# When the weighted sums of the last phase start, and how the first gathers leave

## The reference, cut to what matters

```
scores  = softmax(xt @ Wg.T)                      # 16 experts
topi    = the 4 best experts of the 2 best groups # per token
weights = scores at topi
h   = silu(xt @ W1[e].T) * (xt @ W3[e].T)         # expert e, 352 wide
y   = sum over the 4 chosen e of weights * (h @ W2[e].T)
z   = silu(xt @ Ws1.T) * (xt @ Ws3.T) @ Ws2.T     # shared, 704 wide
out = x + y + z
```

## Time and profile before

| | |
|---|---|
| median of 3 runs | 918.76 us (918.58 to 924.74) |
| the profiled execution | 918.96 us, of which the span is 917.4 us |
| PE busy | 898.6 us, 98% of the span |
| DVE busy | 555.3 us, 61% |
| POOL busy | 494.6 us, 54% |
| ACT busy | 332.5 us, 36% |
| TensorE clock granted | 1.000 over the span |
| in the last phase, 825.65 to 900.85 us | PE busy 75.20 of 75.20 us, DVE 71.00, POOL 56.64 |
| landing of `hblk<-h_d` after its issue | 2.6 us (median of 79) |

### The profile page before, as it was taken

The page is one execution under the profiler, slowest core; times in us unless marked ns, Lnnn a source line. Parts: engine busy times, 40 slices in busy tenths (PEclk is TensorE's granted clock), DMA queues, the critical chain, the costliest instruction groups (busy, mean ns, idle before and its releaser), DMA issues.

```text
span 917.4 us, 19372 instructions
## 1 busy us (share of the span) xinstructions
PE 898.6 (98%) x4966; PEld 804.3 (88%) x4967; DVE 555.3 (61%) x1104; ACT 332.5 (36%) x708; POOL 494.6 (54%) x346
## 2 busy tenths in 40 slices
PE   8999998899999999999999999999999999999998
PEld 5777887688889999999999999999999999989997
DVE  6656667988886644444444444444444444459996
ACT  4556554454324322333323333333333333332221
POOL 1127777874167774434646664456666643137771
PEclk9999999999999999999999999999999999999999
DMA  6729996655579977777878776778878755588883
GB/s 217 259 105 377 392 402 256 230 191 171 185 234 304 304 246 200 226 198 241 254 237 250 250 246 200 236 244 252 256 247 252 250 166 157 162 243 249 269 259 128
DMA packets 180649, 218.97 MB, mean 239 GB/s; under 512 B 56576, under 2 KB 124160, under 8 KB 180224
## 3 DMA queue, kind: packets, MB, share of 16 engines
q1 hardware_dynamic: 118080, 123.50, 42.2%
q0 software_dynamic: 20816, 79.44, 26.2%
q10 hardware_dynamic: 41712, 15.54, 6.3%
HBM read 127.38 MB, written 91.03 MB: 238 GB/s over the span
## 4 chain that ended last, share of the span: by engine, by line
PE 80%; DVE 9%; issue 4%; ACT 3%; DMA 2%; POOL 1%; ACTq 0%; DVEq 0%; SPq 0%; POOLq 0%
PE ps L1173 15%; PE ps L1174 15%; PE ps L1175 15%; PE ps L1232 8%; PE ps L1230 8%; PE ps L1231 8%; PE ps L1022 2%; PE ps L1038 2%; PE ps L969 1%; DVE st L1479 1%; DVE res L1477 1%; PE ps L1058 1%; PE ps L1060 1%; PE ps L1059 1%; DVE st L1294 1%
## 5 line engine op out<-in xcount | busy, mean ns | idle before, releaser
L1173 PE MATMUL ps<-whi,xhi 128*128 (+1 forms) x888 | 287.9, 324 | 1.5 <-DVE xlo L1522 0.8
L1175 PE MATMUL ps<-whi,xlo 128*128 (+1 forms) x888 | 286.0, 322 | 0.0
L1174 PE MATMUL ps<-wlo,xhi 128*128 (+1 forms) x888 | 285.9, 322 | 0.0
L1554 DVE TENSOR_TENSOR hrow<-ps,sg 128x352 f32<-128x352 f32 x95 | 49.8, 524 | 217.8 <-ACT sg L841 212.1
L1173 PEld LDWEIGHTS ps<-whi,xhi 128*128 128x128 f32 x888 | 166.9, 188 | 6.2 <-issue 1.4
L1174 PEld LDWEIGHTS ps<-wlo,xhi 128*128 128x128 f32 x888 | 167.0, 188 | 4.0
L1175 PEld LDWEIGHTS ps<-whi,xlo 128*128 128x128 f32 x888 | 166.6, 188 | 0.0
L841 ACT ACTIVATE sg<-ps 128x352 f32<-128x352 f32 x111 | 51.6, 465 | 275.2 <-PE ps L1175 275.2
L848 ACT ACTIVATE xhi<-ps 128x512 fp32r<-128x512 f32 x112 | 67.0, 598 | 141.2 <-DVE ps L1515 141.1
L569 POOL TENSOR_TENSOR wlo<-raw,whi 128x2816 fp32r<-128x2816 f32 x16 | 100.6, 6289 | 2.4 <-POOL whi L567 0.8
L661 POOL DMA_INDIRECT raw<-yslot_d,sloti x64 | 68.3, 1067 | 55.3 <-DMA yslot_d<-ysb 22.6
(11 more groups left out here) (204 smaller groups left out, 1579.8 us busy)
## 6 DMA issues: line engine op xcount, KB each, us to landing
raw<-wexp_in POOLq DMA_DIRECT2D x18, 2176.0 KB, 11.1
xslot_d<-zero SPq DMA_DIRECT2D x10, 2048.0 KB, 21.5
xg<-xslot_d SPq DMA_DIRECT2D x320, 64.0 KB, 2.1
yslot_d<-ysb SPq DMA_DIRECT2D x80, 256.0 KB, 2.4
h_d<-hrow ACTq DMA_DIRECT2D x79, 192.0 KB, 2.9
hblk<-h_d SPq DMA_DIRECT2D x79, 192.0 KB, 2.6
xg<-xn_d SPq DMA_DIRECT2D x128, 64.0 KB, 3.4
xq<-x_in SPq DMA_DIRECT2D x16, 256.0 KB, 3.3
```

What stands on the lines that cost most here:

```text
L1173: pe.matmul(ps[:, bank, 0:INTER], xh, wh, start=(k == 0), stop=False)
L1174: pe.matmul(ps[:, bank, 0:INTER], xh, wl, start=False, stop=False)
L1175: mm = pe.matmul(ps[:, bank, 0:INTER], xl, wh, start=False, stop=(k == KT - 1))
```

## The change

`LAG` goes from 1 to 0 and `PACE` from 9 to 8: sums 4t to 4t+3, those of tile t, stand in step t, one in each quarter, from step 0 to step 15. On POOL the gathers of tiles 1 to 3 no longer wait until those of the tile before have landed. The gathers of tiles 4 to 15 keep their waits: for the matmuls of `up` three tiles back, and for the sums that free their ring place.

```diff
-LAG, PACE = 1, 9
+LAG, PACE = 0, 8
...
             for t in range(NT):
-                if 1 <= t < GR:
-                    pool.wait_ge(gathered[t - 1], 16 * TOPK)
                 if t >= GR:
                     pool.wait_ge(mm1, 2 + NT + NR + t - 2)
                     pool.wait_ge(comb, TOPK * (t - GR + 1))
```

## The result

The changed kernel takes 922.43 us (median of 22 runs, 919.69 to 926.4), the kernel before, in as many runs beside it, 920.38 us (917.38 to 924.74). The ratio is 1.0026, with a 95% interval of 1.0014 to 1.0037: about 2.4 us slower (the two medians lie 2.05 us apart). The forecast was 1.4 us over the kernel before, whose first three runs had a median of 918.76; with more runs that median moved up by 1.6 us, which has nothing to do with the change.

What follows compares the result with a forecast made beforehand. PE, busy 98% of the span, was taken to set the pace. Profiled 918.96 + 0 + 0 + 1.4 = 920.4 us; with the runs' median 0.2 us lower, the forecast was 920.2 us, range 918.5 to 922.5.

Steps and rivals of the forecast that it cites:

- Middle steps, 0 us: Steps 1 to 14: four sums a step relieve DVE, but PE has no idle time to give back; 0 us.
- Gathers in time for their sums, 0 us: Last phase, tiles 0 to 3: gathers land before their sums want them, all with 5 us or more to spare; 0 us.
- Step 15, +1.4 us: End of last phase: the chain of sums on DVE delays h_low(15), so down(15) starts late; +1.4 us, at least +0.9.
- Step 0, 0 us: Start of last phase: four new sums fit DVE's idle time and PE's slack, so they cost nothing; 0 us.
- the transfers of routed tile 78 land late: Rival near step 0: more gathers in flight slow tile 78's store and load, PE waits 2.9 us, 923.1 us; chance 0.12.
- The rule of the Trainium skill: On the tile 78 rival: engines alternate between queues, so a deeper gather queue slows nothing further; the rival's 2.9 us becomes 0.
- the other reading that I gave: On the tile 78 rival: if engines served transfers in order of issue, its 2.9 us would stand.

Runs made afterwards that it cites:

- one wait back: Changed kernel with tile 1's gathers again waiting for those of tile 0, tiles 2 and 3 free; ratio 1.0002 to the kernel before.
- The sums alone: Kernel before with only the sums moved (LAG 0, PACE 8), gathers of tiles 1 to 3 keeping their waits; ratio 1.0054 to the kernel before.
- the moved tail: Changed kernel with the last two sums of tile 15 put behind h_low(15); ratio 1.0009 to the kernel before.
- the free gathers alone: Kernel before with only the waits of the gathers of tiles 1 to 3 removed, sums as before (LAG 1, PACE 9); ratio 1.0004 to the kernel before.
- the changed kernel again: The changed kernel, unaltered, timed a second time beside the kernel before; ratio 1.0028.

## Why the prediction was right in one place and wrong in another

- *Middle steps, 0 us*: right. With one wait back the stretch up to `tr_h(14)` is 102.6 us against 102.7, with four sums a step instead of four and five. DVE at 71.00 of 75.20 us did not pace PE.
- *Gathers in time for their sums, 0 us*: right for the changed kernel; no sum waits on `raw`. The sums alone show how tight it would have been otherwise.
- *Step 15, +1.4 us*: the mechanism was right, the size a little high. It measured 1.13 to 1.14 us in all five profiles with these sums in this order, and nothing once two sums stood behind `h_low(15)`. The oversized term is the 0.22 us from the end of `h_low` to PE's start, taken from the stop at 807.32; here PE began 0.06 us behind it (917.57 + 0.55 = 918.12, 918.18).
- *Step 0, 0 us*: wrong, and with it the forecast. It cost 4.4, 1.9, 1.5 and 3.2 us in the four profiles with tile 1's gathers free and the whole run of 16 (the changed kernel twice, the moved tail, the free gathers alone). The sums' share of that term was right: alone they cost nothing there. The step that failed is the sentence on the rival "the transfers of routed tile 78 land late": "in 808 to 818 gathers were in flight already when this load ran, so only the depth of their queue changes". True of the load, which took 4.8 us before and 4.3 in the changed kernel; but the store ran from 804.94 to 809.64, its last 1.8 us in a gap of the gathers, and the change closed that gap: 9.8 us instead of 4.7. I had read the load's row and not the store's. The rival was the case that came, with its sign, the `hblk` transpose waiting and PE idle near 820 us; I gave it 0.12. Its price came near by luck: it put 2.5 us on the store and 2.5 on the load, and the runs put 5.1 on the store and none on the load. The sum also took the gathers' own pace as 1.45 us from a row in which they wait for sums; free of waits one left every 1.25 us, which moved nothing in the forecast.
- *The rule of the Trainium skill* ("DMA: Bandwidth & Descriptors", queues, rings and completion order: the engines take turns between queues, a packet at a time) I read as speaking against that rival. Serving in order of issue, the other reading that I gave, is ruled out by the changed kernel: gathers issued from 806.76 to 809.26 us, behind the store's 805.80, had landed by 814.2, at most 4.9 us later, and the store only at 815.6. Whether the turns were one packet each is not shown: q0 and q10 had 687 and 528 packets over the store's 9.8 us, but 395 and 63 of them from 810.8 to 815.3. My error was in the step from the rule to the 0 us, which holds only where the other queue is non-empty in both kernels. For the load it was; for the store's last 1.8 us it was empty before, and here it was made non-empty.
- *Clock*: not in the prediction at all. It cost another 1.6 us in one of the four profiled executions with a stop there, the one with the longest idle time before `tr_h(0)` (1.59 us; 1.42, 0.86 and 0.54 in the others).

What stays open: the four profiles lost 1.5 to 4.4 us at step 0, but the ratios say less on average, 2.4 us in all, of which 1.1 would be the tail, and for the free gathers alone 0.4 us with an interval up to 1.7. The division of the 2.4 us into two causes rests on the profiles. How often the stop comes, and how long it is without a profile being taken, no run here shows.

## What to carry to other kernels

A wait that looks like mere caution may make the gap in which another queue's transfer gets through: before removing one, list every transfer that now overlaps, the stores too, with its slack to the engine that sets the pace, and look at its landing time with and without neighbours. Relieving an engine that is nearly full but never waited for gave nothing back here; instructions put in front of the last thing that the pacing engine needs cost what exceeds its slack, here three sums of about 0.75 us each and 1.13 us of loss. And the halves of a change can depend on each other: here the sums without the free gathers were the slowest kernel.

## What the runs showed of the hardware that I had not expected

- A store of 192 KB in 528 small packets took 2.2 us with only 26 other packets beside it, and with some 850 of SP's 4.7 with 113 gather packets, 6.8 with 375 and 9.8 with 687. In the store of 9.8 us, 465 of its packets moved in the first 5.0. The load of the same data took 4.3 us in the same kernel, issued 9.9 us later.
- After 1.59 and 0.57 us of idle time of PE within 2.7 us, the granted clock went to half about 1 us later and stayed there for some 3.3 us. With 1.42 and 0.42 us of such waits (the free gathers alone) and with 0.86 and 0.59 (the changed kernel again) it stayed at full.
- Where executions differ most is not the last phase: with the same stretch of 109.8 to 110.0 us five profiles have spans from 916.2 to 919.7 us.
